# The setup of a fused four-layer kernel reordered: condition first, masks between the film products, and another opening order of the pieces

## The reference

```python
x = L0(x, cond_2048, mask_BxS_ik0)    # linear attention, 16 heads; softmax of q over a head, of k over time
x = L1(x, cond_2048, mask_BxS_ff1)    # softmax attention, 16 heads of 16, over 256 keys
x = L2(x, cond_2048)                  # two selective scans (forward, backward), 512 channels, 16 states
x = L3(x, cond_2048, mask_BxSx1_fk1)  # linear attention, 8 heads
# L0, L1 and L3 each end in a film block:
e = silu(emb) @ emb_w + emb_b; scale, shift = split(e)
h = silu(layernorm(y) * (1 + scale) + shift) @ out_w + out_b;  return x + h
```

## Time and profile before

| | us |
|---|---|
| median of 3 runs | 4681.6 |
| lowest, highest | 4666.38, 4683.03 |
| the profiled execution | 4666.17 |
| its span | 4664.4 |
| DVE, POOL, PE, ACT busy in it | 4085.4, 3926.7, 3850.9, 3671.9 |
| end of the setup's block | 90.1 |

### The profile page before, as it was taken

The page is one execution under the profiler, slowest core; times in us unless marked ns, Lnnn a source line. Parts: engine busy times, 40 slices in busy tenths (PEclk is TensorE's granted clock), DMA queues, the critical chain, the costliest instruction groups (busy, mean ns, idle before and its releaser), DMA issues.

```text
span 4664.4 us, 73193 instructions
## 1 busy us (share of the span) xinstructions
PE 3850.9 (83%) x26068; PEld 2522.2 (54%) x26068; DVE 4085.4 (88%) x5552; ACT 3671.9 (79%) x8678; POOL 3926.7 (84%) x1836
## 2 busy tenths in 40 slices
PE   4867888888888889888888888888888888888665
PEld 3644555555555555555555555555555555555333
DVE  4313899999999999999999999999999999999985
ACT  0135788888898888888889888888888888888763
POOL 0003899999999999999999999999999999999995
PEclk7777899999999999999999999999999999999876
DMA  4002444444454444445454434445454444444441
GB/s 121 3 7 69 102 100 102 113 110 113 104 119 114 105 98 102 113 110 121 103 115 111 107 93 106 113 110 118 103 119 111 104 97 104 113 113 115 111 106 35
DMA packets 338585, 470.58 MB, mean 101 GB/s; under 512 B 56474, under 2 KB 166150, under 8 KB 338218
## 3 DMA queue, kind: packets, MB, share of 16 engines
q1 hardware_dynamic: 338218, 465.91, 42.9%
HBM read 378.71 MB, written 86.56 MB: 100 GB/s over the span
## 4 chain that ended last, share of the span: by engine, by line
PE 37%; ACT 25%; DVE 20%; POOL 8%; issue 7%; DMA 1%; SPq 0%; DVEq 0%; POOLq 0%; ACTq 0%
PE ps L170 14%; ACT ps L699 7%; DVE ps L714 6%; POOL S_X L758 5%; PE ps L375 5%; PE ps L394 4%; PE ps L793 4%; DVE S_X L714 4%; PE ps L160 3%; DVE A_sm L428 3%; POOL S_X L771 2%; DVE S_X L729 2%; PE ps L403 2%; PE ps L538 2%; ACT T_q L153 1%
## 5 line engine op out<-in xcount | busy, mean ns | idle before, releaser
L758 POOL TENSOR_TENSOR S_X<-S_slot,S_bc 128x1024 f32<-128x1024 f32 x1024 | 2392.0, 2361 | 33.3 <-PE ps L793 28.6
L699 ACT ACTIVATE ps<-S_slot,acol 128x256 f32<-128x256 f32 x4096 | 1736.2, 466 | 184.7 <-DVE S_X L729 127.2
L714 DVE TENSOR_TENSOR_SCAN ps<-ps,S_X 128x512 f32<-128x512 f32 x1088 | 1297.2, 1212 | 64.4 <-ACT ps L699 44.7
L714 DVE TENSOR_TENSOR_SCAN S_X<-ps,S_X 128x512 f32<-128x512 f32 x960 | 1148.7, 1208 | 31.3 <-ACT ps L699 24.8
L771 POOL TENSOR_TENSOR S_X<-S_X,S_bc 128x1024 f32<-128x1024 f32 x480 | 1132.7, 2363 | 49.7 <-DVE S_X L714 49.6
L729 DVE TENSOR_TENSOR S_X<-ps,S_bc 128x512 f32<-128x512 f32 x1088 | 724.0, 676 | 8.9
L793 PE MATMUL ps<-S_X,sum 128*32 128x256 f32 x8192 | 631.8, 412 | 38.8 <-POOL S_X L771 29.1
L394 PE MATMUL ps<-A_qP,A_kP 32*128 32x256 f32 x2048 | 338.2, 454 | 103.4 <-DMA A_qP<-A_ring 62.3
L428 DVE TENSOR_REDUCE A_sm<-ps 128x4 f32<-128x1024 f32 x256 | 312.7, 1222 | 95.9 <-PE ps L375 89.7
L793 PEld LDWEIGHTS ps<-S_X,sum 128*32 128x32 f32 x8192 | 203.0, 114 | 321.1 <-issue 186.4
L375 PE MATMUL ps<-A_kP,A_qP 32*128 32x256 f32 x2048 | 298.2, 409 | 52.4 <-DVE A_sm L428 32.4
(11 more groups left out here) (293 smaller groups left out, 7181.3 us busy)
## 6 DMA issues: line engine op xcount, KB each, us to landing
S_slot<-scr_dd SPq DMA_DIRECT2D x1024, 256.0 KB, 4.5
scr_dd<-C_dd SPq DMA_DIRECT2D x64, 1024.0 KB, 6.8
S_bc<-scr_bc SPq DMA_DIRECT2D x256, 256.0 KB, 6.6
L_xin<-in_x SPq DMA_DIRECT2D x32, 256.0 KB
...
```

The lines of the kernel that those rows point to most:

```text
L699: ins = a.activation(B["bank"][half_at(b, u, i)][:, n * T:(n + 1) * T], B["slot"][:, s, j, 0, :], ACT.Exp, scale=K.k["acol"][:, s, LINES * ...
L714: v.tensor_tensor_scan(line(x if u in ON_POOL else decay), line(decay), line(x), 0.0, ALU.mult, ALU.add).then_inc(S.scan.sem, 1)
L758: g.tensor_tensor(B["X"][:, u % RING], B["slot"][:, s, :, 1, :], rep(B["bc"][:, s, q, :], 1, LINES), ALU.mult).then_inc(S.b.sem, 1)
```

## The change

The setup's loads are issued and counted in finer groups, with the condition as the very first load. DVE, PE and ACT work on the condition ahead of the attention weights; the masks come between L0's film and L1's on DVE and PE. On SP the two trips of the bias row come ahead of the 21 scan loads. In the second block `FIRST` has the same letters of each kind in another order; `TURN` is the same. The computation is the same. The diff (moved lines that stay the same within themselves are cut):

```diff
 
-    names = [L + m for L in ("L0", "L1", "L3") for m in "qkv"] + ["condT"]
-    return names + ["%sf%d" % (L, m) for L in ("L0", "L1", "L3") for m in range(4)] + ["mask%d" % m for m in range(3)]
+    films = {L: ["%sf%d" % (L, m) for m in range(4)] for L in ("L0", "L1", "L3")}
+    names = ["condT"] + [L + m for L in ("L0", "L1", "L3") for m in "qkv"]
+    return names + films["L0"] + ["mask%d" % m for m in range(3)] + films["L1"] + films["L3"]
 
 
...
-LOADS = {"attention": 31, "conditions": 20, "scans": 21}
+LOADS = {"cond": 1, "attention": 31, "L0film": 4, "masks": 3, "L1film": 4, "L3film": 4, "ada": 4, "scans": 21}
...
                 t.count(t.ready().memset(allb[0:1, sections["L1" + m]], 0.0))
+            v.wait_ge(got["cond"], 16 * LOADS["cond"])
+            v.wait_ge(scalar, 3)
+            mark["silu"] = t.count(t.ready().tensor_tensor(M["cond"][:], M["cond"][:], M["sig"], ALU.mult))
+            evict("condT", M["condT"][:], bank("condT")[:, 0:KE * NB].rearrange("p (k b) -> p k b", k=KE))
             t.ready().wait_ge(got["attention"], 16 * LOADS["attention"])
             for L in ATTENTION:
...
 
-            v.wait_ge(got["conditions"], 16 * LOADS["conditions"])
-            v.wait_ge(scalar, 3)
-            mark["silu"] = t.count(t.ready().tensor_tensor(M["cond"][:], M["cond"][:], M["sig"], ALU.mult))
-            evict("condT", M["condT"][:], bank("condT")[:, 0:KE * NB].rearrange("p (k b) -> p k b", k=KE))
             v.wait_ge(round1, 16)
             split(lambda i: M["bparts"][:, i, :], M["rowsb"][:], M["back"][:])
             mark["bparts"] = t.n
             pc, mf, mr = M["pcol"], M["mf"], M["mr"]
-            for L, (_, _, _, _, at) in FILM.items():
-                so = M[L + "so"]
+
+            def film(L):
+                at, so = FILM[L][4], M[L + "so"]
+                v.wait_ge(got[L + "film"], 16 * LOADS[L + "film"])
                 for m in range(4):
                     t.ready().wait_ge(made, place["%sf%d" % (L, m)])
                     mark["%sf%d" % (L, m)] = t.count(v.tensor_scalar(so[:, m, :], bank("%sf%d" % (L, m))[:, 0:NB], M[L + "fb"][:, m:m + 1], 1.0 if m < 2 else 0.0, ALU.add, ALU.add))
                 for i in range(KD):
                     t.count(t.ready().tensor_scalar(pc[:, :, at + i], so[:, i, :], M[L + "fs"][:, i:i + 1], None, ALU.mult))
                     t.count(t.ready().scalar_tensor_tensor(pc[:, :, at + 2 + i], so[:, i, :], M[L + "ft"][:, i:i + 1], so[:, 2 + i, :], ALU.mult, ALU.add))
+
+            v.wait_ge(got["masks"], 16 * LOADS["masks"])
             t.count(t.ready().tensor_copy(mf[:, 0, :], M["mi"][:]))
             t.count(t.ready().tensor_scalar(mr[:, 0, :], mf[:, 0, :], 1.0, NEG0, ALU.is_equal, ALU.mult))
             mark["mf"] = t.count(t.ready().tensor_scalar(mf[:, 0, :], mf[:, 0, :], 1.0, None, ALU.not_equal))
+            film("L0")
             t.count(t.ready().tensor_scalar(mr[:, 1:3, :], mf[:, 1:3, :], -1.0, 1.0, ALU.mult, ALU.add))
             t.count(t.ready().tensor_scalar(mr[:, 1:3, :], mr[:, 1:3, :], NEG1, None, ALU.mult))
             split(lambda i: M["mparts"][:, :, i, :], mr[:], M["mback"][:])
             mark["mparts"] = t.n
             for m, at in ((0, 0), (1, 2), (2, 12)):
                 evict("mask%d" % m, pc[:, :, at:at + 2].rearrange("p b t -> p t b"), bank("mask%d" % m)[:, 0:TT * NB].rearrange("p (t b) -> p t b", t=TT))
+            film("L1")
+            film("L3")
             mark["pcol"] = t.n
             t.ready()
...
 
+            p.wait_ge(masks, mark["ident"])
+            p.wait_ge(vector, mark["silu"])
+            turned("condT", P, [M["cond"][:, i * P:(i + 1) * P] for i in range(KE)])
             p.wait_ge(got["attention"], 16 * LOADS["attention"])
             for L in ATTENTION:
                 for m in "qkv":
                     product(L + m, 1, D, [(M[L + "b"][:, i:i + 1], M[L + m + "raw"][:, i, :]) for i in range(KD)])
-            p.wait_ge(masks, mark["ident"])
-            p.wait_ge(vector, mark["silu"])
-            turned("condT", P, [M["cond"][:, i * P:(i + 1) * P] for i in range(KE)])
             p.wait_ge(vector, mark["condT"])
             for L in FILM:
+                p.wait_ge(got[L + "film"], 16 * LOADS[L + "film"])
                 for m in range(4):
                     product("%sf%d" % (L, m), P, NB, [(M[L + "fw"][:, i, m * P:(m + 1) * P], M["condT"][:, i, :]) for i in range(KE)])
-            p.wait_ge(vector, mark["mf"])
-            for m in range(3):
-                turned("mask%d" % m, P, [M["mf"][:, m, t * P:(t + 1) * P] for t in range(TT)])
+                if L == "L0":
+                    p.wait_ge(vector, mark["mf"])
+                    for m in range(3):
+                        turned("mask%d" % m, P, [M["mf"][:, m, t * P:(t + 1) * P] for t in range(TT)])
             p.wait_ge(made, len(names))
...
-            a.wait_ge(got["conditions"], 16 * LOADS["conditions"])
+            a.wait_ge(got["cond"], 16 * LOADS["cond"])
...
             with nc.allow_non_contiguous_dma(reason="columns of bias vectors, once"):
+                load("cond", M["cond"][:], W["cond_2048"])
                 q.wait_ge(vector, 11)
...
-                load("conditions", M["cond"][:], W["cond_2048"])
                 for L, (w, b, s, t, _) in FILM.items():
-                    load("conditions", M[L + "fb"][:], cols("%s_cond_%s" % (L, b)))
-                    load("conditions", M[L + "fs"][:], cols("%s_cond_%s" % (L, s)))
-                    load("conditions", M[L + "ft"][:], cols("%s_cond_%s" % (L, t)))
-                    load("conditions", M[L + "fw"][:], tiles("%s_cond_%s" % (L, w)))
-                load("conditions", M["mi"][:], W["mask_BxS_ik0"])
-                load("conditions", M["mf"][:, 1, :], W["mask_BxS_ff1"])
-                load("conditions", M["mf"][:, 2, :], W["mask_BxSx1_fk1"].rearrange("b t a -> b (t a)"))
-                load("conditions", M["wada"][:], W["L2_cond_Wada"].rearrange("(m p) k -> p m k", p=P))
-                load("conditions", M["bada"][:], line("L2_cond_bada"))
+                    load(L + "film", M[L + "fb"][:], cols("%s_cond_%s" % (L, b)))
+                    load(L + "film", M[L + "fs"][:], cols("%s_cond_%s" % (L, s)))
+                    load(L + "film", M[L + "ft"][:], cols("%s_cond_%s" % (L, t)))
+                    load(L + "film", M[L + "fw"][:], tiles("%s_cond_%s" % (L, w)))
+                    if L == "L0":
+                        load("masks", M["mi"][:], W["mask_BxS_ik0"])
+                        load("masks", M["mf"][:, 1, :], W["mask_BxS_ff1"])
+                        load("masks", M["mf"][:, 2, :], W["mask_BxSx1_fk1"].rearrange("b t a -> b (t a)"))
+                load("ada", M["wada"][:], W["L2_cond_Wada"].rearrange("(m p) k -> p m k", p=P))
+                load("ada", M["bada"][:], line("L2_cond_bada"))
                 for n, name in enumerate(("norm1_g", "norm1_b")):
-                    load("conditions", M["rows"][:, n, :], W["L2_cond_" + name].partition_broadcast(NB))
+                    load("ada", M["rows"][:, n, :], W["L2_cond_" + name].partition_broadcast(NB))
+                q.wait_ge(vector, mark["allb"])
+                q.dma_start(scr["bias"].rearrange("(a n) -> a n", a=1), M["allb"][:]).then_inc(round3, 16)
+                q.wait_ge(round3, 16)
+                q.dma_start(M["rowsb"][:], scr["bias"].rearrange("(a n) -> a n", n=P)).then_inc(round1, 16)
+                q.wait_ge(vector, mark["bparts"])
+                q.dma_start(scr["bparts"].rearrange("i (a n) -> a i n", n=P), M["bparts"][:]).then_inc(round2, 16)
+                q.wait_ge(round2, 16)
+                q.dma_start(k["bias"][0:PARTS, :], scr["bparts"]).then_inc(stored, 16)
                 load("scans", M["g2"][:], cols("L2_cond_norm2_g"))
...
             assert asked == LOADS, asked
-            q.wait_ge(vector, mark["allb"])
-            q.dma_start(scr["bias"].rearrange("(a n) -> a n", a=1), M["allb"][:]).then_inc(round3, 16)
-            q.wait_ge(round3, 16)
-            q.dma_start(M["rowsb"][:], scr["bias"].rearrange("(a n) -> a n", n=P)).then_inc(round1, 16)
-            q.wait_ge(vector, mark["bparts"])
-            q.dma_start(scr["bparts"].rearrange("i (a n) -> a i n", n=P), M["bparts"][:]).then_inc(round2, 16)
-            q.wait_ge(round2, 16)
-            q.dma_start(k["bias"][0:PARTS, :], scr["bparts"]).then_inc(stored, 16)
             q.wait_ge(vector, mark["mparts"])
             q.dma_start(scr["mask"], M["mparts"][:]).then_inc(stored, 16)
             q.wait_ge(vector, mark["pcol"])
             q.dma_start(scr["pcol"].rearrange("b p n -> p b n"), M["pcol"][:]).then_inc(stored, 16)
+            q.wait_ge(got["ada"], 16 * LOADS["ada"])
             q.wait_ge(stored, 16 * 3)
...
 FIRST = {
     "PE": (
-        "WWWWWWWWWWWWWWWLLLLWLWWWWWLWWLWWWWWWWWWWWWWLWWWWWWLWWWWWWWWWWWWWLAAAAAAAAAAAAAAAAAAAAAAAAAALALLLALLLLLLAAAAAACACAACACACA"
```

(19 more changed lines are left out.)

2 lines of the change are left out of this document (1 added, 1 removed).

## The result

The changed kernel takes 4663.84 us (median of 10 runs, 4639.76 to 4672.39) where the old one, beside it on the same chip, took 4680.05 (10 runs, 4666.03 to 4687.41): ratio 0.9962, 95% interval 0.9945 to 0.998, so 0.38% or 16 us faster. The forecast of 27 us lies between the two, just outside the interval of the first (9 to 26 us) and inside that of the second (23 to 43); the measured time is inside the range, and the sign is right. By the bound of 0.5% the first comparison falls into "within", to which the prediction gave 0.35, and not into "faster", to which it gave 0.6.

What follows compares the result with a forecast made beforehand. No engine bounds the kernel throughout; with the turn unedited, only time taken off the 590 us or so ahead of it counts. 15 + 5 + 4 - 2 + 5 = 27 us, so 4681.6 - 27 = 4654, range 4630 to 4674.

Steps and rivals of the forecast that it cites:

- Part A: Setup: bias rows return earlier and VectorE starts its split sooner; gain 15 us, bounds 4 and 18.
- SP's term: Setup: SP issues the 21 scan loads after the bias round trip, taking 17.3 us, bounds 9.5 and 25.1.
- The landing: Setup: from the columns' store to the barrier's opening, 9.3 us plus 2 for scan loads still in the rings.
- R1: Setup's wait moves to SP: scan loads take 25 us again, setup gains 4 to 6, total 18; chance 0.20.
- Part B: Folding: later folding products cover PE's wait for the first attention's normalized rows; gain 5 us, bounds 2 and 7.
- Part C: First batch's attention beside L1: L1 is normalized inside the softmax, so it transposes earlier; gain 4 us, bounds 1 and 6.
- Part D: A1, C0 and L2: pieces pushed into the exponential chain's gaps; loss 2 us, bounds gain 1 and loss 5.
- R4: Closer-packed pieces hold up PE's clock, giving the folding and ramp some 13 us more, 4641; chance 0.05.
- Part E: First scans: VectorE has already done more scan halves and products by A2's first norm; gain 5 us, at most 9.
- R2: A2's score chain sets the entry to the turn: first scans gain 0, total 19, 4663; chance 0.15.
- R3: Engines enter the turn with other offsets, making a slower rhythm; 1.7 us a turn gives 4708; chance 0.05.
- the 22 us are there at 443 but no 27 at 674: Sign of a wrong prediction: third batch's first norm 22 us early, but the two scans of 674.03 not 27.

Runs made afterwards that it cites:

- e6: New setup, old order up to the third batch's first norm, remaining pieces in the new relative order; 4691.1 us, ratio 0.9988 to the old kernel.
- e1: Changed kernel with the old order of pieces, so the new setup alone; 4663.95 us, ratio 0.9965 to the old kernel.
- e2: Old kernel with the new order of pieces, so the old setup; 4668.23 us, ratio 0.9977 to the old kernel.
- e10: Changed kernel with ScalarE's decays for the scan halves moved between the third batch's softmax exponentials; 4665.93 us, ratio 0.9946 to the old kernel.
- e11: As e10, and PE's pieces between the third batch's first four scores spread as in the old order; 4665.96 us, ratio 0.9941.
- e5: Changed kernel up to the third batch's first norm, every engine's remaining pieces in the old relative order; 4654.07 us, ratio 0.9914 to the old kernel.
- second profile: The changed kernel run again unchanged, beside the old one on another chip; 4657.06 us, ratio 0.9929.
- e3: Changed kernel with six unused products filling PE's pause before the softmax's first product in each batch; 4613.39 us, ratio 0.986 to the old kernel.
- e7: Changed kernel with three pauses of PE filled in each batch by products that no output uses; 4618.79 us, ratio 0.9839 to the old kernel.
- e12: Changed setup, old relative order behind the third batch's first norm, three PE pauses filled only from the third batch on; 4607.93 us, ratio 0.9821.
- e9: Changed kernel with both stores between the scan loads, old order behind the third batch's first norm, three PE pauses filled; 4614.4 us, ratio 0.9834.

## Why the prediction was right, and which step of it failed

- **What bounds the kernel.** Right in the main: what the edit takes off ahead of the turn is carried to the end. At the fourth reciprocal the changed kernel was 17.3 and 24.0 us ahead in its two profiles, and the medians differ by 16 and 35. Over the kernels without fillers the two go together, roughly: leads of -0.7 (e6), 12.0 (e1), 12.2 (e2), 11.9 (e10), 17.5 (e11) and 33.2 us (e5) there, and medians 5, 17, 13, 26, 26 and 42 under the old one's. The sentence "both versions enter it with every engine at the same piece", so that the turn may be left out, was too simple: the turn costs 129.7 to 133 us by the state of PE's clock, 28 times, so two runs of one kernel can differ by 33 us (4639.76 to 4672.39), as much as the change is worth or more.
- **Part A, forecast 15, measured 12.9** (11.6 in the second profile; in the ten the block opens between 76.20 and 79.08). The steps of VectorE were right: split at 42.36 (42.3), scan loads from 45.94 (45.9). SP's term was too small: 20.8 us for the 21 loads, not 17.3, and the columns waited 5 us for it. The landing was put too long: 77.25 - 67.70 = 9.55 us, not 11.3, where the old one took 9.33. One profile is not enough here: in the ten with this order on SP (changed twice, e1, e3, e5 to e7, e10 to e12) it took 9.3 to 11.1 us, 10.2 on the mean, and in the two of the old setup (old, e2) 9.3. R1 was right about the place of the wait and wrong about its size. By the rule of the Trainium skill ("DMA: Bandwidth & Descriptors", Queues, rings and completion order) that the prediction gives, descriptors taken in ring order and a completion counted only after the engine's earlier writes, the store should have landed later behind the loads. The traces agree in direction, by 0.9 us on the mean and 0.2 us in the first profile. The other way round, with the store ahead of seven loads (e9), SP needs 14.7 us to issue them instead of 6.3.
- **Part B, forecast 5, measured 7.0** (19.9 - 12.9); the wait ahead of the transposition is 0.18 instead of 4.15. **Part C, forecast 4:** A1's first maximum is 23.4 us early (333.85 to 310.48), 3.5 more than A0. In the first profile its stretch ran at the clock of 0.69; in the second it was 4.4 us shorter. The size is thus known to 4 us only.
- **Part D, forecast a loss of 2, measured a gain of 4.7** (23.4 to 28.1 us, though three scan halves and two products with C more are done by then). The work pushed into the exponential chain cost nothing that shows: the second reciprocal is 24.1 us early. From there to the norm it takes 41.0 us instead of 45.0, at a granted clock of 0.83 instead of 0.77. Of R4 the direction is confirmed here, and nowhere else in the lead.
- **Part E, forecast a gain of 5, measured a loss of 10.8** (28.1 to 17.3). This is the step that failed, and with the wrong sign: "the turn, with far less idle, shows that VectorE can be kept full". Counting the work that is left says what the stretch could take at least; the idle time isn't a constant to be added to it, it is made by the order. It grew by 8 us in the first 120. The loss lies in the new order behind the third norm: exchanged alone, it costs 12 us (e5) and 9 us (e6) between the second and the fourth reciprocal, and a filled pause gives back 3.6 of them (e3). Which pieces are at fault is open. R2 had the place, and a bound of 0 where it was -11.
- **R3**, another rhythm: the turns' lengths do vary, but by the clock and not by the offsets, and in both directions; the first profile's 0.3 us a turn (131.42 - 131.13) is three long turns more (10, 7) and is no property of the kernel as far as one profile of each can tell. The other changed profile has 14.
- **The sum** came out close (27; 16 and 35 measured) since A, B, C, D and E missed by -2, +2, -0.5, +7 and -16, which makes -10: errors of both signs, and that they cancel this far is luck. By its own signs the prediction names this case as wrong: "the 22 us are there at 443 but no 27 at 674". They were 28.1 and 17.3.
